# An opening of its own for image 0, and image 3's output stage interleaved with attention's start

## The chip, the cores and the metric

One NeuronCore of a Trainium2 chip runs the whole kernel. Its engines are TensorE (PE in the profile; PEld is its weight load), VectorE (DVE), ScalarE (ACT), GpSimd (POOL) and SyncE (SP), which here only issues DMAs. Each has a queue of its own and executes it in order; semaphores order the engines among each other. The metric is the device time of one execution in microseconds, lower is better.

## The reference

The input is 4 images of 32 x 32 tokens with 384 channels. For each image:

```python
x = x + L0(_gn(x))      # group norm, selective scan layer
x = x + L1(_gn(x))      # group norm, attention

# L0, with DI = 192, N = 16, K = 4 directions, L = 1024 tokens
xh, z = split(x @ in_proj_w.T)
xc    = silu(depthwise_conv3x3(xh) + conv_b)
xs    = [rows, columns, rows reversed, columns reversed] of xc
dts, Bs, Cs = split(einsum(xs, x_proj_w));  dts = softplus(dts @ dt_w + dt_b)
h = h * exp(dt * A) + (dt * u) * B;  y = sum_n(h * C) + D * u      # over 1024 tokens
y = layernorm(sum of the 4 directions) * g + b
return (y * silu(z)) @ out_proj_w.T

# L1: 12 heads of 32, rotary q and k, relative position bias by row and column, softmax, projection
```

All of it is fp32, apart from B/C rows that are split into three bf16 parts.

## The kernel before, in words

Activations lie with channels on partitions and 1024 tokens along the free dimension. PSUM has 8 banks of 512 fp32; `banks(k, n)` names n of them from k. In the scan stage they are `JOB` (0, 1: every matrix product of the input and output stages and of dt), `C_PSUM` (2, 3), `DA` (4, 5) and `Y_PSUM` (6, 7). SBUF is an arena of slots of 1024 columns which are reused.

**Scan stage.** The 4 x 192 rows of (direction, channel) of an image are 6 tiles of 128 (`SEQ`), with 16 states each (`NST`): 96 items per image (`ITEMS`). An item is a pass over the engines: SyncE broadcasts a row of B (`load_b`, L473), GpSimd multiplies by it (`times_b`, L1599, a ring of `R3` = 3), ScalarE computes the decay into `DA` (`decay`, L1442), VectorE scans (`scan`, L1081), TensorE spreads the row of C (`c_product`, L568), VectorE multiplies by it (`times_c`, L1089), and TensorE adds it to `Y_PSUM` (`accumulate`, L577). Softplus for the next tile takes seven ScalarE steps (`soft`, L1410 to L1433) and GpSimd's `delta` (L1576 to L1583) and `times_u` (L1589).

**Front.** The input stage of an image (`front`) is cut into jobs: group norm statistics (`stats`, `moments`, `var`, `rstd`, `norm`), the product `xh` (channels 0 to 127 of xh), `pad` (the remaining 64, as two image halves with padding rows), nine taps of `conv` for either part, the copies `acc` that add conv_b, SiLU in steps `sig` (Exp, Ln, Exp on ScalarE), `cap` and `u` or `gate` on GpSimd, turned copies `ucopy`, the product `z`, and the products `dts` and `bc` of x_dbl, of which B and C are stored and split (`brows`, `bchi`, `split`, `bcmid`, `rest`, `bclo`). **Mid** is the output stage of an image: `y` (three orders added and centred), `yf`, `sq`, `var`, `rstd`, `scale`, `affine`, `gate`, `out` (six half products), `add`, group norm 2, and stores of `x1` and `xn2` to DRAM.

Tables such as `PE_FRONT`, `ACT_MID` give each job of an engine an item at which it is issued into the queue of that engine. For image f the jobs fall into the scan of image f - 1; `*_FIRST` are the tables for image 1, whose jobs fall into image 0's scan, and negative times lie in the scan before that. For image 0 there is no scan to run beside, so each engine runs `in_order(*_FRONT)` for image 0 ahead of its loop, with the same jobs, the same engines and all PSUM uses in `JOB`. SyncE loads x, then eight small columns and `group_mean` on one semaphore (`columns`), `w_in` and the other matrices; TensorE, VectorE and ScalarE wait for all columns at first. `front(0, "next_x")` loads image 1's x after z, `z_store`, `b_store` and `bcs` follow, and only then the first `load_b`.

**The seam.** For image 3 there is no next scan: after the last item each engine runs `in_order(*_MID)` for image 3. Only then attention begins, image by image. Its start follows `START` and `JOBS[0]`: four projections of q and k (`proj`, L561), eight value blocks (`v`, L814, banks 0 to 3), two relative products by column (`rel`, L854) and two by row (`relh`, L843); rotary steps are on VectorE (L1125, L1126) and GpSimd (L1629, L1636). SyncE loads the operands of each head (`operands`, L534) as they get ready. Then come the scores (L880), the biased minimum (L1201), the exponential (L1526), the turning (L891) and the weighing (L905). In the kernel before, SyncE stores x1 and xn2 of image 3 and waits for both before it loads x1 of image 0 and issues head operands.

## Time and profile before

| | us |
|---|---|
| median of 3 runs | 3094.7 (3093.93 to 3096.32) |
| profiled execution | 3094.16 |
| its span | 3092.4 |
| first scan begins | 131.16 |
| last accumulation ends | 1634.97 |
| attention's first scores begin | 1737.13 |
| PE, DVE busy share of the span | 87%, 73% |
| ACT, POOL busy share of the span | 52%, 44% |

The profiled execution took 0.5 us less than the median, and its span is 1.8 us shorter than its time; times below are counted from the start of the span. A timeline row gives the start, the duration, the engine, the line, the operation, what it writes and reads, and in brackets how long the engine had been idle before it and who ended that. In a row that merges several instructions (x12) the duration runs from the first one's start to the last one's end. A fp32 product of 512 columns appears as two matmuls.

### The profile page before, as it was taken

How to read it: one execution, taken by the hardware profiler on the slowest of the kernel's cores; microseconds unless marked ns; L12 is line 12 of the kernel's file. 1: busy time of each engine (PE TensorE's matmuls, PEld its weight loads, DVE VectorE, ACT ScalarE, POOL GpSimd, SP SyncE). 2: the span in 40 equal slices, each digit the busy share in tenths (PEclk: the TensorE clock that was granted, in tenths of full speed). 3: DMA queues.
4: the chain of work that ended last, by engine and by line, in shares of the span. 5: the costliest groups of instructions: out<-in, count | busy, mean ns of one | idle time of the engine just before them, and what ended most of it. 6: DMA issues, size and time to landing. Idle time of an engine off the chain costs nothing. (4 is left out here: it accounts for less than half of the span.)

```text
span 3092.4 us, 40835 instructions
## 1 busy us (share of the span) xinstructions
PE 2684.6 (87%) x16088; PEld 1346.6 (44%) x16088; DVE 2242.5 (73%) x2157; ACT 1614.7 (52%) x1972; POOL 1351.2 (44%) x624
## 2 busy tenths in 40 slices
PE   5579788988889878687767999999999999999999
PEld 2134233333333333232322565555555565556555
DVE  0398988899888998899992566646665566646665
ACT  2464655555555556555541456625564356525564
POOL 1577887887778877788670200011000300011000
PEclk9799999999999999999996999999999999999999
DMA  2344544455444555445551210120120210120110
GB/s 78 108 142 129 163 150 144 150 140 168 165 145 148 142 170 167 154 160 140 197 172 36 76 36 18 39 75 1 36 56 14 63 36 22 35 76 1 35 36 22
DMA packets 93526, 297.03 MB, mean 96 GB/s; under 512 B 16172, under 2 KB 18872, under 8 KB 93208
## 3 DMA queue, kind: packets, MB, share of 16 engines
q1 hardware_dynamic: 93336, 294.43, 30.8%
q8 instruction: 128, 2.10, 0.3%
q14 instruction: 62, 0.51, 0.1%
HBM read 238.27 MB, written 23.07 MB: 85 GB/s over the span
## 5 line engine op out<-in xcount | busy, mean ns | idle before, releaser
L1599 POOL TENSOR_TENSOR arena<-arena 128x1024 f32<-128x1024 f32 x384 | 903.2, 2357 | 307.4 <-DVE arena L1081 297.7
L1081 DVE TENSOR_TENSOR_SCAN arena<-PS,arena 128x1024 f32<-128x1024 f32 x384 | 879.0, 2289 | 102.2 <-ACT PS L1442 70.9
L577 PE MATMUL PS<-arena,ident 128*128 128x512 f32 x1536 | 762.0, 620 | 15.0 <-ACT arena L1453 12.8
L1442 ACT ACTIVATE PS<-arena,a_inf,a_neg 128x1024 f32<-128x1024 f32 x384 | 463.8, 1208 | 586.3 <-DVE arena L1081 580.3
L1201 DVE CUSTOM_DVE_ANT_1 arena<-PS,arena 128x1024 f32<-128x1024 f32 x384 | 467.7, 1219 | 323.4 <-PE PS L880 321.8
L1526 ACT ACTIVATE arena<-arena,neg_max 128x1024 f32<-128x1024 f32 x384 | 441.0, 1148 | 494.8 <-DVE neg_max L1201 494.8
L1089 DVE TENSOR_TENSOR arena<-arena,PS 128x1024 f32<-128x1024 f32 x384 | 460.8, 1200 | 57.7 <-PE PS L568 56.4
L568 PE MATMUL PS<-arena,sel 96*128 96x512 bf16 x768 | 239.4, 394 | 295.5 <-DVE arena L1089 291.7
L1629 POOL TENSOR_TENSOR arena<-arena 128x512 f32<-128x512 f32 x48 | 68.4, 1425 | 955.2 <-ACT arena L1495 955.2
L880 PE MATMUL PS<-arena 64*128 64x512 f32 x1536 | 431.6, 640 | 19.3 <-DMA arena<-arena 12.8
L577 PEld LDWEIGHTS PS<-arena,ident 128*128 128x128 f32 x1536 | 302.5, 198 | 275.0 <-issue 221.4
L891 PE MATMUL PS<-ident,arena 128*128 128x128 f32 x3072 | 414.7, 278 | 3.8 <-ACT arena L1526 3.6
L891 PEld LDWEIGHTS PS<-ident,arena 128*128 128x128 f32 x3072 | 334.9, 142 | 154.9 <-issue 92.5
L568 PEld LDWEIGHTS PS<-arena,sel 96*128 96x128 bf16 x768 | 55.9, 100 | 577.5 <-DVE arena L1089 503.3
L1155 DVE COPY arena<-PS 128x1024 f32<-128x1024 f32 x192 | 233.9, 1218 | 60.6 <-PE PS L891 57.2
L905 PEld LDWEIGHTS PS<-arena 128*32 128x32 f32 x6144 | 157.0, 110 | 134.0 <-issue 131.7
L905 PE MATMUL PS<-arena 128*32 128x128 f32 x6144 | 206.5, 276 | 0.0
L1503 ACT ACTIVATE arena<-PS 128x1024 f32<-128x1024 f32 x192 | 192.7, 1004 | 19.4 <-PE PS L891 19.4
L880 PEld LDWEIGHTS PS<-arena 64*128 64x128 f32 x1536 | 116.5, 185 | 88.5 <-issue 59.0
L1636 POOL TENSOR_TENSOR arena<-arena 128x512 f32<-128x512 f32 x48 | 64.0, 1333 | 176.3 <-DVE arena L1126 175.7
L561 PE MATMUL PS<-normed,arena 128*128 128x512 f32 x288 | 135.7, 615 | 0.6 <-DVE g_tmp L1025 0.6
L577 PE MATMUL PS<-arena 128*128 128x512 f32 (+1 forms) x224 | 108.3, 622 | 12.0 <-ACT arena L1305 5.5
(125 smaller groups left out, 2205.3 us busy)
## 6 DMA issues: line engine op xcount, KB each, us to landing
arena<-b_rows SPq DMA_DIRECT2D x256, 512.0 KB, 3.7
arena<-b_rows SPq DMA_DIRECT2D x256, 256.0 KB, 3.9
arena<-arena SPq DMA_DIRECT2D x192, 128.0 KB, 3.3
arena<-arena SPq DMA_DIRECT2D x120, 64.0 KB, 2.6
normed<-x_in SPq DMA_DIRECT2D x12, 512.0 KB, 5.4
residual<-x_in SPq DMA_DIRECT2D x12, 512.0 KB, 5.6
x<-residual SPq DMA_DIRECT2D x12, 512.0 KB, 5.3
xn<-residual SPq DMA_DIRECT2D x12, 512.0 KB, 4.7
```

The source lines that it names most:

```text
L568: last = pe.matmul(dst[:, half(h)], lhs, rhs(h), start=(k == 0), stop=(k == len(pairs) - 1))
L577: last = pe.matmul(dst[:, half(h)], lhs, rhs[:, half(h)], start=start, stop=stop, skip_group_check=True)
L880: last = pe.matmul(scores_place(s)[:, h * HALF:(h + 1) * HALF], QX[rows, j, qb * P:(qb + 1) * P], KX[rows, j, :], start=True, stop=True)
L891: last = pe.transpose(turned_place(s)[:, t * P:(t + 1) * P], PR[s % 3][:, t * P:(t + 1) * P], idn)
L905: last = pe.matmul(banks(6, 1)[HD * j:HD * j + HD, (n % 2) * P:(n % 2 + 1) * P], V[:, t, head * HD:(head + 1) * HD], PT[:, n % 2, j, t, :] ...
L1081: dve.tensor_tensor_scan(HS[:, at % 2, ::step], DA[:, ::step], DBU[:, at % R3, ::step], 0.0, ALU.mult, ALU.add).then_inc(scan_done.sem, 1)
L1089: dve.tensor_tensor(HC[:, at % R_HC, :], HS[:, at % 2, :], C_PSUM, ALU.mult).then_inc(hc_ready.sem, 1)
L1155: dve.tensor_copy(PT[:, n % 2, s % HG, :, :], turned_place(s).rearrange("p (t q) -> p t q", t=QB)).then_inc(pt_saved[0].sem, 1)
L1201: dve.tensor_tensor_reduce(out=PR[s % 3].rearrange("p (h w) -> p h w", w=IMG), in0=scores_place(s).rearrange("p (h w) -> p h w", w=IMG), i ...
L1442: act.activation(DA, DELTA[:, tile % 2, :], ACT.Exp, bias=a_inf[:, col:col + 1], scale=a_neg[:, col:col + 1]).then_inc(da_ready.sem, 1)
L1526: act.activation(PR[s % 3], PR[s % 3], ACT.Exp, bias=neg_max[:, s % 4:s % 4 + 1], scale=-1.0, accum_out=row_sum[:, qb, at:at + 1]).then_in ...
L1599: pool.tensor_tensor(DBU[:, at % R3, :], DU[:, tile % 2, :], BSB[:, at % R3, :], ALU.mult).then_inc(dbu_ready.sem, 1)
```

## The change

**Image 0's front.** The functions `front` stay, but each engine gets an ordered list instead of the table for image 0 (`PE_BEGIN`, `DVE_BEGIN`, `ACT_BEGIN`). `job_place` puts pad and bc of image 0 in banks 2 and 3, conv and z in banks 4, 5 and 6, 7; xh and dts stay in `JOB`. The waits are made finer: `mean_loaded`, `w_in_loaded`, one increment for each normalised tile, conv 0 waits for XH and conv 1 for XP, the first product of `dts` needs only `U01`. In SyncE's queue group_mean and w_in are ahead of the columns. `prepare_columns` and `negate_a` follow the group norm. The caps, the products `u`, the turned copies, `brows`, `bchi`, `bcmid`, the three `delta` steps and the first `times_u` of image 0 go to VectorE (`begin`). The gate of z (`sig` 2 and 3, `cap` 2 and 3, `gate`) moves into items 1 to 17 of image 0's scan, `bcs`, `next_x` and `z_store` to items 3 and 24 of SyncE's loop. The table for image 1 has its group norm and `xh` two items later, and XH of image 1 also waits for `z_gated`.

**The seam.** For image 0 of attention, TensorE, VectorE and ScalarE run a list each (`PE_BOTH`, `DVE_BOTH`, `ACT_BOTH`) in which numbers are the jobs of attention's start and names with `v` value blocks, and the others are mid jobs of image 3. Value blocks of image 0 use banks 2 and 3 alternately. `zs` of image 3 is in slots 14 and 15 instead of 19 and 20. GpSimd does the gates after its first four rotary halves; SyncE stores x1 ahead of the `rel` operands and xn2 after them, and loads x1 of image 0 last.

The diff, cut to its core:

```diff
-PE_FIRST = {**PE_FRONT, ("stats",): 4, ("xh", 0): 12, ("xh", 1): 12.5, ("xh", 2): 13, ("pad", 0): 21, ("pad", 1): 21.5,
+PE_FIRST = {**PE_FRONT, ("stats",): 6, ("xh", 0): 14, ("xh", 1): 14.5, ("xh", 2): 15, ("pad", 0): 21, ("pad", 1): 21.5,
             ("pad", 2): 22}
...
+ACT_FIRST = {**ACT_FRONT, ("rstd",): 10.2, ("norm", 0): 11, ("norm", 1): 12, ("norm", 2): 13, ("xh",): 17.5, ("pad",): 25,
...
+PE_BEGIN = ([("stats",)] + [("xh", k) for k in range(CT)] + [("pad", k) for k in range(CT)]
+            + [("conv", m, j) for m in range(2) for j in range(9)]
+            + [("dts", 0), ("z", 0, 0), ("z", 0, 1), ("z", 0, 2), ("dts", 1), ("dts", 2), ("dt",),
+               ("bc", 0), ("bc", 1), ("bc", 2), ("z", 1, 0), ("z", 1, 1), ("z", 1, 2)])
+DVE_BEGIN = [("stats", 0), ("stats", 1), ("stats", 2), ("moments",), ("var",), ("columns",), ("cap", 0), ("u", 0),
+             ("ucopy", 0), ("ucopy", 1), ("cap", 1), ("u", 1), ("ucopy", 2), ("ucopy", 3), ("brows",), ("bchi",),
+             ("delta", 0), ("split",), ("bcmid",), ("delta", 1), ("delta", 2), ("times_u",)]
+ACT_BEGIN = ([("rstd",), ("norm", 0), ("norm", 1), ("norm", 2), ("xh",), ("pad",), ("a_neg",), ("acc", 0),
+              ("sig", 0, 0), ("sig", 0, 1), ("sig", 0, 2), ("acc", 1), ("sig", 1, 0), ("sig", 1, 1), ("sig", 1, 2),
+              ("z", 0), ("dts",)] + [("soft", step) for step in range(SOFT_STEPS)] + [("z", 1), ("bclo",)])
+ACT_ZERO = {("sig", 3, 0): 1.5, ("sig", 2, 0): 2, ("sig", 3, 1): 11, ("sig", 3, 2): 11.5, ("sig", 2, 1): 12,
+            ("sig", 2, 2): 12.5}
+POOL_ZERO = {("cap", 3): 5, ("cap", 2): 6, ("gate", 1): 16, ("gate", 0): 17}
+SP_ZERO = {("bcs",): 3, ("next_x", 0): 3.1, ("next_x", 1): 3.2, ("next_x", 2): 3.3, ("z_store",): 24}
...
+        def job_place(f, what, part=0):
+            if f:
+                return JOB
+            return {"pad": banks(2), "conv": (banks(4), banks(6))[part], "z": (banks(4), banks(6))[part],
+                    "bc": banks(2)}[what]
...
+            return slot(14 + j) if m == B - 1 else ZS[:, j, :]
...
+        PE_BOTH = ([0, 1, ("y", 0, 0), ("y", 0, 1), ("y", 0, 2), 2, ("y", 1, 0), ("y", 1, 1), ("y", 1, 2), 3, ("v", 0),
+                    ("var", 0), ("var", 1), ("v", 1), ("v", 2), 4, ("v", 3), ("v", 4), ("out", 0), ("out", 1), 5, ("v", 5),
+                    ("out", 2), ("out", 3), 6, ("out", 4), ("out", 5), 7, ("v", 6), ("stats",), ("v", 7)])
+        DVE_BOTH = ([0, 1, 2, 3, ("scale", 0), ("scale", 1), 4, ("add", 0), ("add", 1), 5, ("add", 2), ("add", 3), 6,
+                     ("add", 4), ("add", 5), ("add", 6), ("moments",), 7, ("var",)])
+        ACT_BOTH = ([0, 1, ("yf", 0), ("sq", 0), 2, ("yf", 1), ("sq", 1), 3, ("v", 0), ("rstd",), ("v", 1), ("v", 2),
+                     ("affine", 0), ("affine", 1), ("v", 3), ("v", 4), ("v", 5), ("v", 6), ("rstd2",), ("v", 7),
+                     ("norm", 0), ("norm", 1), ("norm", 2)])
+        def v_bank(b, t):
+            return banks(t % 4 if b else 2 + t % 2, 1)
...
+            load_mats({"group_mean": KEPT["group_mean"]}, mean_loaded)
+            load_mats({"w_in": SCAN_MATS["w_in"]}, w_in_loaded)
             for name in COLS:
                 sp.dma_start(COL[name][:, :], cols[name]).then_inc(columns.sem, 16)
-            load_mats({"group_mean": KEPT["group_mean"]}, columns)
-            load_mats({"w_in": SCAN_MATS["w_in"]}, first_mats)
...
+                    for job in due(SP_ZERO, i) if b == 0 else ():
+                        front(0, *job)
...
+                    if b == 0 and k == 2:
+                        for part in range(CT):
+                            mid(B - 1, "x1_store", part)
...
+                if b == 0:
+                    for part in range(CT):
+                        mid(B - 1, "xn2_store", part)
+                    sp.wait_ge(x1_stored.sem, x1_stored.at(CT * B))
+                    sp.wait_ge(xn2_stored.sem, xn2_stored.at(CT * B))
+                    load_image(X[:, :, :], x1, b, x_loaded.sem)
...
+                    pe.wait_ge(xn_normed.sem, xn_normed.at(CT * f + k + 1))
...
+                    if j == 0 and f == 0:
+                        ready = (xh_saved, xp_saved)[m]
+                        pe.wait_ge(ready.sem, ready.at(1))
...
+                    if f == 0 and which == 0:
+                        ready = u_ready if k else u_gated
+                        pe.wait_ge(first_mats.sem, first_mats.at(len(SCAN_MATS) - 1))
+                        pe.wait_ge(ready.sem, ready.at(1))
+                    elif f == 0 and k == 0:
...
+                for entry in PE_BOTH if b == 0 else ():
+                    if isinstance(entry, int):
+                        if entry == 2:
+                            pe.wait_ge(y_saved.sem, y_saved.at(3 * B))
+                        job(0, entry)
+                    elif entry[0] == "v":
+                        for k in range(CT):
+                            value_product(entry[1], k)
+                    else:
+                        mid(B - 1, *entry)
+                if b == 0:
+                    pe.wait_ge(gn2_var.sem, gn2_var.at(B))
+                    pe.wait_ge(onehot_loaded.sem, onehot_loaded.at(2 * HG))
...
+                elif what == "cap":
+                    which, = args
+                    dve.wait_ge(sig_exp.sem, sig_exp.at(SIGMOIDS.index(which) + 1))
+                    dve.tensor_scalar(sig_home(which), sig_home(which), EXP_CAP, None, ALU.min
+                                      ).then_inc(sig_capped.sem, 1)
+                elif what == "u":
+                    m, = args
+                    dve.wait_ge(sig_ready.sem, sig_ready.at(m + 1))
+                    dst, src = ((U01[:, 0, :], ACC[:, 0, :]), (ACC[:, 1, 0:HALF], ACC[:, 1, 0:HALF]))[m]
+                    dve.tensor_tensor(dst, src, sig_home(m), ALU.mult).then_inc(u_gated.sem, 1)
...
+                    if k < 2:
+                        dst, src = ((u1[XT:P, :], U01[0:XT, 0, :]), (u2[0:XT, :], U01[XT:P, 0, :]))[k]
+                        dve.tensor_copy(grid(dst), by_column(src))
+                        return
...
+                    if f == 0 and which >= 2:
+                        if which == 3:
+                            act.wait_ge(b_stored.sem, b_stored.at(2))
+                        else:
+                            act.wait_ge(bc_lo.sem, bc_lo.at(1))
...
+                        act.wait_ge(z_gated.sem, z_gated.at(2 * f))
...
-                front(0, *job)
-            for step in range(3):
-                delta(0, step)
-            times_u(0)
+            front(0, "rest")
...
+                    if b == 0 and n == 4:
+                        for job in in_order(POOL_MID):
+                            mid(B - 1, *job)
```

## Rows read from the trace of the kernel before

**Rows 1.** Timeline, end of the opening: start us, us, engine line op, idle before.

```profile
105.76 1.23 DVE L1044 TENSOR_TENSOR arena<-PS,arena 128x1024 f32<-128x1024 f32 x1 [83.90 <-ACT arena L1358]
...
111.27 1.10 ACT L1410 ACTIVATE arena<-PS,dt_b 128x1024 f32<-128x1024 f32 x1
...
121.34 2.34 POOL L1579 TENSOR_TENSOR arena<-arena 128x1024 f32<-128x1024 f32 x1
...
131.16 2.29 DVE L1081 TENSOR_TENSOR_SCAN arena<-PS,arena 128x1024 f32<-128x1024 f32 x1 [23.79 <-POOL arena L1599]
```

**Rows 2.** Timeline, VectorE, two neighbouring scans late in image 3.

```profile
1606.07 2.29 DVE L1081 TENSOR_TENSOR_SCAN arena<-PS,arena 128x1024 f32<-128x1024 f32 x1 [0.16 <-ACT PS L1442]
...
1609.63 2.29 DVE L1081 TENSOR_TENSOR_SCAN arena<-PS,arena 128x1024 f32<-128x1024 f32 x1 [0.16 <-ACT PS L1442]
```

**Rows 3.** Timeline between the last item and attention's first exponential.

```profile
1631.37 3.60 PE L577 MATMUL PS<-arena,ident 128*128 128x512 f32 x8
...
1667.57 24.11 PE L561 MATMUL PS<-arena,w_out 128*128 128x512 f32 x24 [9.52 <-POOL arena L1569]
...
1699.80 3.50 ACT L1260 ACTIVATE residual<-residual,g_bias,g_rstd 128x1024 f32<-128x1024 f32 x3
...
1737.13 2.85 PE L880 MATMUL PS<-arena 64*128 64x512 f32 x12 [0.58 <-ACT arena L1483]
...
1739.58 1.15 ACT L1526 ACTIVATE arena<-arena,neg_max 128x1024 f32<-128x1024 f32 x1 [2.50 <-DVE neg_max L1201]
```

**Rows 4.** Timeline, attention's start in image 1: first projections, first scores.

```profile
2047.98 10.46 PE L561 MATMUL PS<-normed,arena 128*128 128x512 f32 x24
...
2083.66 2.85 PE L880 MATMUL PS<-arena 64*128 64x512 f32 x12 [0.58 <-ACT arena L1483]
```

**Rows 5.** Busy us of each engine in two windows, then PEclk, DMA share, GB/s.

```profile
1652.00:1658.00 6.00, 6.00 (x8) 1.60 (x7) 0.00 (x0) 0.00 (x0) 0.00 (x0) 0.58 0.00 0
...
1740.00:2032.00 292.00, 286.85 (x2845) 170.94 (x2846) 193.94 (x283) 168.40 (x267) 20.14 (x16) 1.00 0.10 27
```

**Rows 6.** Timeline, the opening from the loads to z.

```profile
0.72 1.35 SPq L413 DMA_DIRECT2D normed<-x_in  x3
...
13.30 3.66 DVE L1010 BATCH_NORM_STATS2 bn<-normed 128x6 f32<-128x512 f32 x6 [1.86 <-ACT a_neg L1239]
...
18.16 3.11 PE L586 MATMUL PS<-mv,group_mean 128*128 128x2 f32 x14 [18.16 <-DMA arena<-centre_in]
...
26.71 7.87 PE L577 MATMUL PS<-normed,arena 128*128 128x512 f32 x12 [5.44 <-ACT normed L1260]
...
35.70 3.12 PE L633 MATMUL PS<-normed,arena 128*64 128x480 f32 x24 [1.11 <-ACT arena L1325]
...
40.15 15.09 PE L609 MATMUL PS<-arena 128*128 128x512 f32 x36 [1.34 <-ACT arena L1331]
...
56.44 6.14 PE L609 MATMUL PS<-arena 128*128 128x512 f32 x14 [1.20 <-ACT arena L1268]
...
62.42 1.85 PE L609 MATMUL PS<-arena,last_taps 128*128 128x512 f32 x4
...
65.05 5.42 PE L577 MATMUL PS<-normed,arena 128*128 128x512 f32 x12 [0.78 <-ACT arena L1268]
```

**Rows 7.** Transfers into the tile normed until 25 us, issue to landing.

```profile
DMA to landing us min/median/max: 3.2/4.1/5.8
```

**Rows 8.** Groups by form, VectorE, attention of image 0: busy, mean ns.

```profile
L1172 DVE TENSOR_SCALAR arena<-arena,b_qkv 128x512 f32<-128x512 f32 x5 | 2.4, 487 | 0.2
```

**Rows 9.** Timeline, the gate of image 0's z: Exp on ScalarE, cap on GpSimd.

```profile
83.25 1.06 ACT L1283 ACTIVATE arena<-arena 64x1024 f32<-64x1024 f32 x1
...
84.40 2.76 POOL L1543 TENSOR_SCALAR arena<-arena 64x1024 f32<-64x1024 f32 x1 [9.80 <-ACT arena L1283]
```

**Rows 10.** Page, DMA issues: count, KB each, median us to landing.

```profile
arena<-arena SPq DMA_DIRECT2D x120, 64.0 KB, 2.6
...
x<-residual SPq DMA_DIRECT2D x12, 512.0 KB, 5.3
```

More of the change, by code:

```diff
@@ L661, in front @@
                     c0, rows = ((DI, P), (DI + P, XT))[part]
[L662 removed]
+                    last = add_halves(job_place(f, "z", part)[0:rows, :], W["w_in"][:, k, c0:c0 + rows], XN[:, k, :],
+                                      k == 0, k == CT - 1)
                     if k == CT - 1:
@@ L1090, in times_c @@
                                   ).then_inc(hc_ready.sem, 1)
-            for job in in_order(DVE_FRONT):
-                front(0, *job)
+            for job in DVE_BEGIN:
+                begin(*job)
+            dve.wait_ge(prep.sem, PREPARED_BY - 1)
             dve.wait_ge(consts.sem, consts.at(N_CONST))
@@ L1340, in front @@
                     rows = (P, XT)[part]
-                    act.activation(ZS[0:rows, part, :], JOB[0:rows, :], ACT.Copy).then_inc(z_saved.sem, 1)
+                    act.activation(ZS[0:rows, part, :], job_place(f, "z", part)[0:rows, :], ACT.Copy).then_inc(z_saved.sem, 1)
                 elif what == "acc":
```

222 lines of the change are left out of this document (139 added, 83 removed).

## The prediction

> **What bounds the kernel now.** I read the profile in this order: first the timeline until the first scan, since nothing can overlap a scan stage that has not begun; then two neighbouring items of the scan loop; then the stretch between the last scan and the first attention scores; last the busy time and the granted clock of a few windows.
>
> The loop of 4 x 96 items starts with the scan of item 0 at 131.16 us, after VectorE was idle for 23.79 us; everything before it is the serial opening of image 0 [rows 1]. In the loop an item takes 3.56 us (two scan starts): decay on ScalarE, scan 2.29 and the product with C on VectorE, 0.16 us of waiting [rows 2]. It is a cycle of its own: a later first scan shifts everything behind it by as much, so the opening counts one for one. TensorE's last accumulation ends at 1631.37 + 3.60 = 1634.97, and attention's first scores begin at 1737.13, its first exponential at 1739.58 [rows 3]: 102.2 us in which the output stage of image 3 runs first and attention's start second. There the 24 output matmuls take 24.11 us [rows 3], against 10.46 us for 24 projections of image 1 [rows 4]: in the window 1652 to 1658 the granted clock averages 0.58, TensorE drops from 2.4 to 1.2 GHz [rows 5]. Attention itself keeps TensorE busy 286.85 of 292 us at clock 1.00 [rows 5]; the edit leaves it alone.
>
> **Part A, the opening.** The chain before ran through all of the front: each PSUM use waited for ScalarE to empty JOB, and SiLU steps went ScalarE, GpSimd, ScalarE, GpSimd. I rebuild it step by step with the new order, in us from the start of the span:
> - Loads. The third x tile is issued near 1.6 and lands at most 5.8 later, at 7.4 [rows 6, 7]. Before, VectorE waited until the small columns and group_mean had landed too and began its statistics at 13.30 [rows 6]. They now follow each tile: the last third of 3.66 us ends at 8.7. Moments take the 1.2 us that lie between the statistics' end and the first matmul: 9.9. I keep the 3.11 us of the statistics matmuls: 13.0. The matrices are issued right behind x, some 4 us earlier than now, so I let nothing wait for them; a miss costs about 1 us.
> - The gap 18.16 + 3.11 to 26.71 is 5.4 us of variance, root and three normalisations; TensorE now waits for one of three (3.50 / 3 = 1.2 each, [rows 3] has the same line in the later norm), so 5.4 - 2.3 = 3.1: 16.1. Product xh 7.87 (its first matmuls slow, kept): 24.0. Pad 3.12: 27.1; it needs no wait, as it has banks of its own, and saving XH lies beside it. Convolution 0, 15.09: 42.2; saving XP falls beside it. Convolution 1, 6.14 + 1.85 = 8.0, again in banks of its own: 50.2 [rows 6].
> - SiLU of half 0 runs beside convolution 1: bias copy 1.1, Exp 1.1, cap, Ln 1.1, Exp 1.1, product 1.2 from 42.2, ready at 48.7 with a cap of 0.9. The first x_dbl product (a third of 5.42) then runs at once: 52.0. z part 0 (12 matmuls, 5.42): 57.4. Beside it SiLU of half 1 and the four turned copies, now on VectorE. VectorE's full-width TENSOR_TENSOR takes 1.23 us [rows 1]; no row shows its copy from SBUF with turned strides. The nearest is TENSOR_SCALAR on half the length, 0.49 us [rows 8]. Lower bound 0.5 us for each half length, upper bound 1.23 for each full one. From convolution 1's end at 50.2: copy, Exp, cap, Ln, Exp, product, halves of 0.5 to 0.7, give 54.0; the copies of half 1 add 1.4 to 2.8: 55.4 to 56.8. Both lie under 57.4, so z hides them and the term is 0; I take the upper bound, as strides can only slow a copy. Without this cover they would cost up to 3 us.
> - The other two thirds of x_dbl 3.6: 61.0. Copy 1.1: 62.1. dt product 1.8: 63.9. Softplus 121.34 - 111.27 = 10.1 [rows 1]: 74.0. The B/C product (5.4) runs beside it until 69.3, then VectorE has brows, bchi, delta 0 and split at 1.23 each: 74.2; bcmid 1.2: 75.4; delta 1, delta 2, times_u, 3 x 1.2: 79.0. On GpSimd three such products cost 2.34 each [rows 1]. The first product with B stays on GpSimd, 2.34: 81.4. The B rows are stored from 70.5 on, and land before 79. z part 1, bclo and the bcs loads end near 83, when the product with C of item 0 asks for them behind scan 1: no wait of size.
>
> First scan at 81.4 instead of 131.16: **49.8 us**. The Trainium skill ("VectorE: DVE Perf Modes", the perf-mode tier table) says that a copy or tensor_scalar of fp32 from SBUF runs at two elements a cycle and any PSUM source at one. The 0.49 us for 512 agrees; by it the turned copies take their lower bound and, being hidden, change nothing, while bcmid ends 0.6 us sooner, which would give 50.4.
>
> **What the opening gives back.** Gate z of image 0 is not removed but moved into items 1 to 17: on ScalarE six passes of 1.06, on GpSimd two caps of 2.76 [rows 9] and two products of 2.34. ScalarE's decay (1.2) must follow each scan at once, so an item holds 3.56 us of its work. Items 11 and 12 get decay 1.2, Ln and Exp 2.2, and a normalisation of 1.2 for image 1: 4.6, so 1.0 over, twice. Elsewhere it fits. GpSimd runs up to two items ahead: 6 us of slack; the caps fall in items slowed by statistics, the products right behind the four delta products, where I count a lag of 5.4 to 5.8, just covered. XH of image 1 now also waits for these gates, ScalarE's decay being next in its queue; by my count 0.4 us to spare. bcs and next_x stand before the fourth B load on SyncE's queue, which may cost 0 to 3. I take 3 in all, bounds 2 and 12. Part A: 49.8 - 3 = **47**.
>
> **Part B, the seam.** TensorE gets one list with both works, and banks 2, 3 for values, so I sum its work. Attention's start alone takes 2083.66 - 2047.98 = 35.7 us in image 1, at full clock [rows 4]. To it come two y products as z's, 2 x 5.42; variance, 8 matmuls of 0.45, 3.6; 24 output matmuls 10.5; statistics 1.6 (half of the 3.11 at 1.2 GHz). Sum 62.2, so it ends at 1697.2, and the last value copy gives scores at 1697.7.
>
> Is the dependent chain shorter? y 0 ends at 1645.9, its square 2.0 later; projection 2 covers that. y 1 ends at 1654.2, variance at 1662.5. Ln and Exp on PSUM 2.1, scale 1.2, affine 1.25 twice with a value copy ahead, gates 2 x 2.32 on GpSimd: yg_ready at 1672.9. TensorE has v 1, v 2, rel 0, v 3, v 4 meanwhile and arrives at 1673.3. So it holds with 0.4 us in hand, and a microsecond more in that chain is a microsecond lost. Behind the output products the statistics end at 1695, and ScalarE must do three normalisations (3.50, [rows 3]) before its first exponential: 1697.7 + 3.5 = 1701.2 instead of 1739.58. That, not the scores, sets the gain: 38.4, **38**. In the queue of SyncE the three x1 stores stand before the eight rel loads of heads 0 to 3; the last store is released at the sixth addition, about 1690.8, and a load of 64 KB lands in 2.6 us, a store in 5.3 [rows 10]. So head 0 is there near 1694 to 1697, under TensorE's arrival, and the norms wait for the store until 1696.2, also under it. zs moves to other slots and costs nothing.
>
> Sum: 47 + 38 = 85. The profiled execution took 3094.16 us, 0.5 below the median of 3094.7, so 3094.7 - 85 = 3009.7, say **3010**.
>
> **Rivals.**
> (1) The deferred gates and the SyncE order cost more than 3 us in the item loop. If none of it is covered: ScalarE 6.5, GpSimd 10.2 minus what the slack takes, up to 15: **3022**. For it: GpSimd's lag is within 1 us of its slack. Against: at most two items overflow on ScalarE by my count.
> (2) The seam's side work ends last: rel loads behind x1 stores, or the gate chain. Each has under 1 us in hand, and loads share the queues with 1.5 MB of stores: 3 to 8 us, **3015**.
> (3) TensorE's clock drops in the seam as before. From 1653 on some 43 us of work at 2.4 GHz remain; at 1.2 GHz part B brings nothing: **3048**. For it: the row at 0.58 [rows 5]. Against: before it came two pauses of 2 us per 5.4 of work; the new list has none.
> (4) Slower than before: attention of image 0 starts at the lower level and stays there. Its 286.85 busy us [rows 5] would double; it decides once more than 85 us of it run at 1.2 GHz, and in full gives **3297**. Against: the clock was back at 1.00 in that window after a far longer drop.
> (5) Opening shorter than summed, as statistics matmuls and xh run warm and x lands at 4 us: **3001**.
>
> **How the numbers follow.** Chances: forecast 0.60, (1) 0.13, (2) 0.12, (3) 0.05, (4) 0.02, (5) 0.08. Range 2998 to 3028: it takes in the upper bound of the give-back, (1), (2) and (5), and leaves out (3) and (4) and tails. A measurement tells 0.2%, 6 us; all but (4) lie far below, faster 0.97, same 0.01, slower 0.02.
>
> **What would show it.** First scan at 80 to 83; TensorE nearly without gaps from 16 to 61 at clock 1.00; VectorE idle on ScalarE around items 11 and 12, 1 us each. Scans of image 1 begin 45 to 49 us sooner. From the last accumulation to the first exponential 66 us instead of 104.6, granted clock 1.00 throughout, the first output product 38 us behind it. It would be wrong if a window there shows 0.5, if the first scores wait for a DMA, or if item times above 3.6 add up to more than 12 us in image 0.

## The result, and where the time went

The changed kernel took 3015.28 us (median of 4 runs, 3011.24 to 3019.43) against 3095.51 us of the kernel before on the same chip (3093.93 to 3096.33): ratio 0.9741, 95% interval 0.9725 to 0.9758, 80 us faster. The forecast was 3010 us, range 2998 to 3028. Its profiled execution took 3011.24 us with a span of 3009.5. Two later sets of runs of the same kernel gave 3018.14 (0.9753, interval 0.9739 to 0.9768) and 3016.24 (0.9763, interval 0.975 to 0.9777).

The profiled executions differ by 82.9 us. The scans mark off the stretches; the times are differences of starts in the timelines:

| stretch | before | after | saved |
|---|---|---|---|
| start of the span to the first scan | 131.16 | 82.40 | 48.8 |
| image 0's scan stage | 370.82 | 374.75 | -3.9 |
| images 1 and 2 | 763.92 | 759.11 | 4.8 |
| image 3, to its last scan | 361.56 | 361.52 | 0.0 |
| last scan to attention's first exponential | 112.12 | 78.54 | 33.6 |
| first exponential to the end | 1352.82 | 1353.18 | -0.4 |

The 4.8 us of images 1 and 2 are not the edit's, as shown below. Without them the change is worth 78 us: 45 of 47 forecast in the opening, 33.6 of 38 in the seam.

The opening after, timeline, all engines; columns as in [rows 1]:

```profile
10.48 3.12 PE L636 MATMUL PS<-mv,group_mean 128*128 128x2 f32 x14 [10.48 <-DVE mv L1160]
...
16.86 7.68 PE L627 MATMUL PS<-normed,arena 128*128 128x512 f32 x12 [3.26 <-ACT normed L1401]
...
24.47 3.12 PE L686 MATMUL PS<-normed,arena 128*64 128x480 f32 x24
...
27.51 20.96 PE L659 MATMUL PS<-arena 128*128 128x512 f32 x50
...
51.72 5.31 PE L627 MATMUL PS<-normed,arena 128*128 128x512 f32 x12
...
54.18 0.86 DVE L1117 COPY arena<-arena 64x512 f32<-64x512 f32 x2
...
55.05 1.23 DVE L1119 COPY arena<-arena 64x512 f32<-64x512 f32 x2
...
73.67 0.69 DVE L1130 CAST arena<-arena 128x1024 bf16<-128x1024 f32 x1
...
74.44 3.03 POOL L1711 TENSOR_TENSOR arena<-arena 128x1024 f32<-128x1024 f32 x1 [74.02 <-DVE arena L1130]
75.61 2.95 DVE L1143 TENSOR_TENSOR arena<-arena 128x1024 f32<-128x1024 f32 x1
...
82.40 2.29 DVE L1225 TENSOR_TENSOR_SCAN arena<-PS,arena 128x1024 f32<-128x1024 f32 x1
```

TensorE goes from product xh to pad and to all 54 tap matmuls (50 in the row shown, 4 behind it) with no idle bracket; in [rows 6] pad and both convolutions had a bracket of 1.1 to 1.3 us that named ScalarE. The turned copies end at 56.28, before z does at 57.03. The oddity is the pair at 74.44 and 75.61: VectorE's `delta` 2 took 2.95 us where its other full-width products took 1.23 [rows 1], and GpSimd's subtraction 3.03 where it took 2.34.

The seam, by windows of the same work: the end of the last accumulation to the first exponential, kernel before, then after. Columns: length, busy us of PE, PEld, DVE, ACT, POOL with counts, PEclk (1.00 is 2.4 GHz, 0.50 is 1.2 GHz), DMA share, GB/s.

```profile
1635.00:1739.60 104.60, 84.75 (x282) 39.35 (x282) 26.94 (x38) 21.57 (x30) 17.26 (x10) 0.76 0.24 76
```

```profile
1585.30:1656.30 71.00, 69.83 (x282) 34.98 (x281) 25.35 (x38) 21.28 (x29) 17.24 (x10) 0.95 0.28 75
```

This pair is the seam in one look. TensorE has 282 matmuls in both. Its idle time fell from 104.60 - 84.75 = 19.9 us to 1.2, which is 18.7 of the 33.6 gained. The other 14.9 are busy time of the same matmuls, which a clock of 0.95 instead of 0.76 shortened: the pauses had cost their own length and, as I read it, the clock behind them. The clock is still not at 1.00, and this is most of what made 33.6 of the forecast's 38. PE rows of the seam after, and ScalarE's at its end:

```profile
1611.71 4.14 PE L883 MATMUL PS<-arena,normed 128*128 128x384 f32 x12
1615.68 3.92 PE L923 MATMUL PS<-arena 128*128 128x32 f32 x32
1619.42 5.55 PE L883 MATMUL PS<-arena,normed 128*128 128x384 f32 x12
1624.81 4.18 PE L611 MATMUL PS<-arena,w_out 128*128 128x512 f32 x8
1628.92 3.77 PE L923 MATMUL PS<-arena 128*128 128x32 f32 x32
1632.51 3.87 PE L883 MATMUL PS<-arena,normed 128*128 128x384 f32 x6
...
1653.28 2.03 PE L949 MATMUL PS<-arena 64*128 64x512 f32 x8 [0.78 <-ACT arena L1632]
...
1652.92 3.49 ACT L1401 ACTIVATE residual<-residual,g_bias,g_rstd 128x1024 f32<-128x1024 f32 x3
...
1656.32 1.13 ACT L1682 ACTIVATE arena<-arena,neg_max 128x1024 f32<-128x1024 f32 x1
```

```profile
1615.70:1618.90 3.20, 3.20 (x31) 3.20 (x29) 0.62 (x1) 2.75 (x3) 1.26 (x1) 1.00 0.11 41
1618.90:1622.30 3.40, 3.40 (x9) 2.19 (x9) 0.69 (x1) 0.00 (x0) 3.40 (x2) 0.50 0.00 0
...
1633.00:1636.20 3.20, 3.20 (x6) 1.62 (x5) 0.41 (x1) 0.00 (x0) 0.00 (x0) 0.53 0.00 0
1636.20:1653.00 16.80, 16.30 (x107) 7.56 (x105) 8.41 (x20) 2.61 (x9) 0.00 (x0) 1.00 0.50 141
```

Two value blocks (L883) are too long: 5.55 instead of 4.14 us for 12, 3.87 instead of 2.2 for 6. Each stands right behind a column-wise relative block (L923, 32 matmuls of 32 columns), and in each the granted clock is 0.50, with TensorE busy in every part of the window. The first fall came at 1618.90, with the last narrow matmuls of the block. "Busy" is a weak word here: idle time under 0.15 us gets no bracket, and the narrow matmuls follow each other every 0.11 us where 384 columns take 0.33. In the kernel before these 32-column matmuls were woven, four at a time, between value matmuls; in the list of the seam each block runs in one piece.

### The profile page after: what moved, and what is told of

Read it like the earlier page. It is cut to its first block and busy times, and to the rows that moved or that the text cites. A ratio compares the mean times of both kernels' runs of the same rounds, so it can differ in the third digit from the quotient of the medians.

```text
span 3009.5 us, 40839 instructions
## 1 busy us (share of the span) xinstructions
PE 2660.0 (88%) x16088; PEld 1337.4 (44%) x16088; DVE 2259.1 (75%) x2174; ACT 1603.2 (53%) x1962; POOL 1334.7 (44%) x616
## 5 line engine op out<-in xcount | busy, mean ns | idle before, releaser
L1298 DVE COPY arena<-PS 128x1024 f32<-128x1024 f32 x192 | 233.8, 1218 | 60.9 <-PE PS L960 57.4
```

## Experiments

Times in this section, unless said otherwise, come from the profiled execution, cut at the scans as above.

**Do the two parts stand alone?** Each part was taken alone. `opening_only` is the changed kernel with the old seam (a), `seam_only` the old kernel with the new seam (b):

```diff
 (a)
+            for job in in_order(PE_MID):
+                mid(B - 1, *job)
...
-                for m, blocks in START if b else ():
+                for m, blocks in START:
 (b)
-            for job in in_order(PE_MID):
-                mid(B - 1, *job)
...
+                for entry in PE_BOTH if b == 0 else ():
...
-                for m, blocks in START:
+                for m, blocks in START if b else ():
```

> The opening, the table for image 1 and the moved gates as in the changed kernel, the seam as before. If the two parts add up: 48.8 us at the first scan, minus 3.9 in image 0's scan, so about 3050 us (ratio 0.9855), with the seam at 104.6 us from the last accumulation to the first exponential and its granted clock falling to 0.50 again. Rival: the 4.8 us that images 1 and 2 were shorter in the changed kernel belong to the opening's shift; then the same items 63 to 67 of image 1 and 71, 84 of image 2 are shorter here and the time is near 3045. If they are a matter of when TensorE's clock happens to drop, these items differ from run to run.

Measured: 3050.24 us (ratio 0.9857, interval 0.9842 to 0.9872), 44 us below before; first scan at 82.38, image 0's stage 375.33, last scan to first exponential 109.38.

> The opening as before, the seam as in the changed kernel. If the parts add up: 33.6 us from the last scan to the first exponential, so about 3062 us (ratio 0.989), first scan at 131.2. In the seam the granted clock should drop to 0.50 twice for 2 to 3 us, each time behind a block of 32 narrow matmuls of a rel job, if those blocks are the cause; if the drops come from a moment in time they fall elsewhere or not at all. If image 1 and 2 stay at 385 and 379 us, the 4.8 us go with the opening; if they are shorter here too, they are spread between runs.

Measured: 3056.31 us (0.9878, interval 0.9862 to 0.9895), 38 us below before; first scan 129.82, image 0's stage 370.55, last scan to first exponential 75.18. 44 + 38 = 82 against 76 to 80 for both: they add, with a remainder of 2 to 6 us. The profiles show two parts of it. In `opening_only` the old seam took 109.38 instead of 112.12 us, 2.7 less, since its long stretch at half clock (0.50 from 1615.7 to 1660.1, in the kernel before from 1653.0 to 1704.2) was 7 us shorter; and `seam_only` had a seam without a fall of the clock. The longer stage of image 0 belongs to the opening alone. The seam by itself was 3.4 us shorter than within the change: here the same unbroken blocks ran with the clock at 1.00.

`after_again` is the changed kernel once more, in the same set:

> The changed kernel once more. Its four runs lay between 3011.2 and 3019.4 us, the one with a profile being the fastest. Theory: the opening (first scan 82.4) and the seam (71.0 us) repeat within 0.5 us, and the spread lies in the scan stage of images 1 and 2, in which TensorE's clock drops at varying items: a slower run shows it there, with a lower mean clock. Rival: the spread lies in the seam, whose two clock drops are long in some runs and short in others; then the seam of this profile differs from 71.0.

Measured: 3018.14 us. First scan 83.03, image 0's stage 375.35, seam 76.86, images 1 and 2 385.26 and 381.13 us instead of 382.42 and 376.69. The same kernel thus differs by 7.3 us in images 1 and 2, which is the 4.8 us above. One item of image 1, the changed kernel's first profile, then `after_again`:

```profile
709.94 1.88 PE L627 MATMUL PS<-arena,ident 128*128 128x512 f32 x4
...
709.90:711.90 2.00, 1.92 (x5) 0.58 (x4) 2.00 (x2) 0.00 (x0) 2.00 (x2) 1.00 0.61 229
```

```profile
713.76 3.62 PE L627 MATMUL PS<-arena,ident 128*128 128x512 f32 x4
...
713.70:717.40 3.70, 3.70 (x6) 1.31 (x5) 3.27 (x5) 1.86 (x6) 3.70 (x2) 0.50 0.87 225
```

The four accumulating matmuls took 3.62 us at 1.2 GHz instead of 1.88 at 2.4 GHz, and the item 4.89 instead of 3.80. The clock falls at such items of an image in some executions and not in others; it did in the kernel before as well (image 1 385.17, image 2 378.75). So nothing in images 1 and 2 is counted for or against the edit.

**Why is the seam 5 us longer than summed?** My theory: the clock falls behind 32 narrow matmuls in a row. The rival: the side chain or the loads of head 0 end last (the prediction's rival 2), and the clock only fills time that would be waited anyway. `seam_mix` weaves the relative blocks into value blocks again and shifts value blocks toward them:

```diff
-                    ("var", 0), ("var", 1), ("v", 1), ("v", 2), 4, ("v", 3), ("v", 4), ("out", 0), ("out", 1), 5, ("v", 5),
-                    ("out", 2), ("out", 3), 6, ("out", 4), ("out", 5), 7, ("v", 6), ("stats",), ("v", 7)])
+                    ("var", 0), ("var", 1), ("v", 1), ("v", 2), ("job", 4, (3, 4)), ("out", 0), ("out", 1),
+                    ("job", 5, (5, 6)), ("out", 2), ("out", 3), 6, ("out", 4), ("out", 5), 7, ("v", 7), ("stats",)])
```

> In the seam the value blocks 3 and 4 are woven between the lines of rel 0, and 5 and 6 between those of rel 1, as in the later images, and v 7 comes ahead of the statistics with its copy ahead of the normalisation. Theory: unbroken runs of matmuls with 32 moving columns let the clock fall, though TensorE is busy throughout; woven it stays at 1.00, v 3 and v 4 take 3.9 instead of 5.4 us and v 5 1.9 instead of 3.7: 3.3 us less, and 0.6 from the copy that no longer stands ahead of the norms, the seam at about 67.1 us, the time some 3.9 us below the changed kernel. Rival: the drops come from the moment or from what stands ahead of the rel blocks; then they stay, and only the 0.6 us is gained.

Measured: 3019.77 us (0.9756, interval 0.9741 to 0.977), seam 76.53. The clock was 1.00 through both blocks, as the theory has it, but the gain did not arrive. The chain of waits of `seam_mix` (start, us, what) and its PE rows there:

```profile
1651.78 0.70 DVE residual L1207
...
1652.50 0.32 SPq L462
...
1654.80 5.44 DMA arena<-arena
...
1660.28 3.70 PE PS L949 x8
```

```profile
1654.87 1.69 PE L636 MATMUL PS<-mv,group_mean 128*128 128x2 f32 x14
1657.24 2.08 PE L949 MATMUL PS<-arena 64*128 64x512 f32 x4 [0.67 <-DVE g_tmp L1170]
1660.28 3.70 PE L949 MATMUL PS<-arena 64*128 64x512 f32 x8 [0.96 <-DMA arena<-arena]
```

The last addition (L1207) releases the last x1 store on SyncE's queue (L462), behind which the `rel` loads of the heads stand; one issued at 1654.80 landed 5.44 us later, scores waited 0.96 us for it, and ran at half clock (3.70 us for 8, 2.03 in the seam above). That is a part of rival 2 at work, once the time in front of it shrinks. It costs behind the first exponential, a stretch that took 1355.59 us here and 1353.18 in the change. It does not set the seam's length of 76.53: the first exponential began at 1661.86, as the three norms ended (1658.45 + 3.51), and these follow the statistics. This edit had also put value block 7 ahead of the statistics, which made them 1.9 us later (62.05 us behind the last accumulation, 60.12 in `seam_mix2`). `seam_mix2` keeps the weaving, leaves blocks 6 and 7 where they were and puts the loads ahead of the stores:

```diff
-                    ("var", 0), ("var", 1), ("v", 1), ("v", 2), 4, ("v", 3), ("v", 4), ("out", 0), ("out", 1), 5, ("v", 5),
+                    ("var", 0), ("var", 1), ("v", 1), ("v", 2), ("job", 4, (3, 4)), ("out", 0), ("out", 1), ("job", 5, (5,)),
...
-                    if b == 0 and k == 2:
-                        for part in range(CT):
-                            mid(B - 1, "x1_store", part)
...
                 if b == 0:
+                    for part in range(CT):
+                        mid(B - 1, "x1_store", part)
```

> Seam alone changed against the changed kernel: v 3 and v 4 woven into rel 0, v 5 into rel 1, the rest of TensorE's order as it was, and SyncE issues the rel operands ahead of the three x1 stores. Theory: both losses of seam_mix go. No clock drop: last scan to first exponential 75.2 us, as in the run of the seam alone that had no drop, against 76.9 and 78.5 in the two of the changed kernel. No wait of the first scores for a DMA, so the stretch behind the first exponential returns from 1355.6 to about 1353. Rival: the rel operands land late for another reason (their own issue, 0.8 us each for 8), then the wait stays; or the norms wait for the later stores and the first exponential moves by 1 to 3 us.

Measured: 3017.57 us (0.976, interval 0.9745 to 0.9775), seam 75.17. Windows over its two woven blocks, and its first scores:

```profile
1622.00:1632.00 10.00, 10.00 (x52) 6.91 (x50) 2.40 (x3) 3.73 (x5) 4.66 (x2) 1.00 0.06 22
1634.00:1642.00 8.00, 8.00 (x44) 5.31 (x42) 1.98 (x3) 0.49 (x1) 0.00 (x0) 1.00 0.00 0
...
1657.30 2.85 PE L948 MATMUL PS<-arena 64*128 64x512 f32 x12 [0.78 <-ACT arena L1633]
```

No window below 1.00, no DMA in a bracket. The seam is 3.4 us shorter than in the change, the theory's amount, and as long as in `seam_only`, which has the stores ahead of the loads: the order of the stores did nothing for it. The stretch behind the first exponential took 1354.28 instead of the 1353 that I expected. The median shows no gain; images 1 and 2 happened to be the long kind again (385.16, 381.13).

The rival form of the theory is that the seam, not the block, is special. `plain_rel` therefore unweaves the blocks at the start of attention's images 1 to 3, and leaves the seam alone:

```diff
-        START = [(m, ()) for m in range(4)] + [(None, (0, 1)), (4, (2, 3)), (5, (4, 5)), (6, ()), (7, ()),
+        START = [(m, ()) for m in range(4)] + [(None, (0, 1)), (4, ()), (None, (2, 3)), (5, ()), (None, (4, 5)), (6, ()), (7, ()),
```

> The changed kernel, but in images 1 to 3 the value blocks stand behind the two rel jobs instead of between their lines: the same matmuls in another order, six more unbroken blocks of 32 narrow matmuls. If unbroken narrow blocks let the clock fall, some of the six are followed by a stretch at 0.50 (in the seam it was two of two, one of two and none of two), and each such drop costs 1.5 to 2 us; attention's start in these images had none in any profile. If the seam's drops came from something else in the seam, all six stay at 1.00.

Measured: 3013.73 us in one run, which says nothing at this size. Of the six unbroken blocks in images 1 to 3 one was followed by the drop (0.50 from 2328.3 to 2331.7):

```profile
2324.89 3.75 PE L923 MATMUL PS<-arena 128*128 128x32 f32 x32
2328.46 5.73 PE L883 MATMUL PS<-arena,normed 128*128 128x384 f32 x12
```

In the new seam, by kernel, one profiled execution each:

| seam | kernels | blocks followed by a drop |
|---|---|---|
| 78.54 | the change, plain_rel, rest_on_dve | 2 of 2 each |
| 78.54 | after_third | 1 of 2, 6.8 us long (value block 7.03 us) |
| 76.86 | after_again, warm, gates_early | 1 of 2 each |
| 75.18 | seam_only | 0 of 2 |
| 75.17 | woven: seam_mix2, all_four | 0 of 2 each |
| 76.53 | woven: seam_mix, with the late statistics | 0 of 2 |

The length of the seam follows the drops: one stretch of 3.4 us at half clock adds 1.7 us, two such stretches or the long one of `after_third` add 3.4. An unbroken block makes a drop possible, not certain (10 of 16 in the seam, 1 of 6 elsewhere); none came at a woven one. What it is in the block that lets the clock fall was not tested: the narrowness, or gaps too short for a bracket.

**What did the last microsecond of the opening cost?** The stretched pair at 74.44 and 75.61 suggests that GpSimd and VectorE keep each other from SBUF. `rest_on_dve` gives the subtraction to VectorE, in front of the products:

```diff
-             ("delta", 0), ("split",), ("bcmid",), ("delta", 1), ("delta", 2), ("times_u",)]
+             ("delta", 0), ("split",), ("bcmid",), ("rest",), ("delta", 1), ("delta", 2), ("times_u",)]
...
+                elif what == "rest":
+                    dve.wait_ge(bc_mid.sem, bc_mid.at(1))
+                    dve.tensor_tensor(REST, REST, BCP[:, 1, :], ALU.subtract).then_inc(bc_last.sem, 1)
...
-            front(0, "rest")
```

> Image 0's second subtraction for the bf16 parts (rest) goes from GpSimd to VectorE, ahead of delta 1. In the changed kernel GpSimd ran it from 74.44 to 77.47 while VectorE's delta 2 took 2.95 us instead of 1.22. Theory: the two slow each other when both read and write SBUF; alone on VectorE, rest and delta 2 take 1.2 each, and the first scan comes 0.5 to 0.8 us earlier, at 81.7. Rival: delta 2 is slow for another reason; it stays near 2.95 and the first scan comes 1.2 us later, at 83.6.

Measured: 3013.9 us in one run; first scan at 81.11, 1.3 us sooner than in the change. Most of that is the front's: its pad matmuls began at 23.63 instead of 24.47, and that start varies from 23.61 to 25.09 among the kernels whose front is unchanged. From the pad matmuls to the first scan these take 57.9 us (82.40 - 24.47 = 57.93; the change run again 57.94 twice), and `rest_on_dve` 81.11 - 23.63 = 57.48: 0.45 us sooner, with one instruction more on VectorE.

```profile
73.56 1.23 DVE L1133 TENSOR_TENSOR arena<-arena 128x1024 f32<-128x1024 f32 x1
74.70 1.22 DVE L1142 TENSOR_TENSOR arena<-arena 128x1024 f32<-128x1024 f32 x1
...
76.03 1.23 DVE L1146 TENSOR_TENSOR arena<-arena 128x1024 f32<-128x1024 f32 x1
...
81.11 2.29 DVE L1228 TENSOR_TENSOR_SCAN arena<-PS,arena 128x1024 f32<-128x1024 f32 x1
```

With the other engine still, `delta` 2 (L1146) took 1.23 again, 1.7 less, of which the added instruction takes back 1.2. The Trainium skill ("SBUF — State Buffer", section "SBUF: two separate sides") says that a VectorE operation with two SBUF inputs and a GpSimd one that reads SBUF take turns over a shared pair of ports, each for the whole instruction. The rows of the change agree for VectorE: 75.61 + 2.95 - 1.22 = 77.34, within 0.2 us of the end of GpSimd's instruction at 77.47. GpSimd's loss, 0.7 us, is smaller than the 1.06 us for which the product before it (74.28, 1.22 us) still ran; no run here shows why.

**Can the slow first matmuls be warmed?** `warm` adds matmuls on zeros whose results nothing reads, six products while x is loading and three behind the statistics:

```diff
+            def keep_warm(n):
+                for _ in range(n):
+                    pe.matmul(banks(2, 1), XP[:, 0:P], XP[:, 0:HALF], start=True, stop=True, skip_group_check=True)
...
+            keep_warm(6)
...
+                if job == ("stats",):
+                    keep_warm(3)
```

> Six matmuls of zeros into banks 2 before TensorE's first wait and three between the statistics and xh; results unused. Theory: the statistics' 3.12 us and the slow start of xh (7.68 instead of 5.3) are TensorE at 1.2 GHz after idling, and can be bought back with work in the idle time: statistics near 1.7, xh near 5.3, first scan 3.8 us earlier, 78.6. Rival: matmuls on zeros, or so early, do not raise the clock, or three of them outlast the gap: no gain, or up to 1.5 us lost.

```profile
1.68 6.93 PE L846 MATMUL PS<-arena 128*128 128x512 f32 x12 [1.68 <-DVE arena L1088]
10.43 2.07 PE L636 MATMUL PS<-mv,group_mean 128*128 128x2 f32 x14 [1.82 <-DVE mv L1168]
12.37 5.47 PE L846 MATMUL PS<-arena 128*128 128x512 f32 x6
17.62 5.71 PE L627 MATMUL PS<-normed,arena 128*128 128x512 f32 x12
```

For comparison, windows of the change over its statistics matmuls and the slow start of xh:

```profile
10.48:13.60 3.12, 3.11 (x14) 3.03 (x14) 0.00 (x0) 0.00 (x0) 0.00 (x0) 1.00 0.98 333
16.86:20.00 3.14, 3.14 (x4) 1.48 (x5) 0.00 (x0) 2.11 (x2) 0.00 (x0) 1.00 0.89 252
```

Measured: 3013.8 us (0.9743, interval 0.9726 to 0.9759), first scan at 81.2, 1.2 us sooner than in the change where I had expected 3.8; the pad matmuls began at 23.27, barely ahead of the 23.61 to 25.09 of unchanged fronts. The first group did its work: statistics matmuls 2.07 instead of 3.12. Then the clock fell all the same, to 0.50 from 11.6 to 18.4: behind 1.82 us without matmuls, during the two-column ones, and before the three fillers began at 12.37. So these ran at 1.2 GHz themselves, took 5.47 us and outlasted the gap that they were to fill, and xh began at 17.62 instead of 16.86. It made up for that with 5.71 instead of 7.68. The theory's "at 1.2 GHz" is not what the record of the clock says of the change, as the two windows above read 1.00; only the spacing of the matmuls speaks for it (xh 0.85 us apart at first, 0.43 at its end, the latter as in other stretches at 1.00).

**Is the give-back in items 11 and 12?** Two scans of the change with more than 0.9 us of idle time before them, and what ScalarE did:

```profile
126.86 1.06 ACT L1435 ACTIVATE arena<-arena 64x1024 f32<-64x1024 f32 x1
127.82 1.23 ACT L1401 ACTIVATE normed<-normed,g_bias,g_rstd 128x1024 f32<-128x1024 f32 x1
128.95 1.19 ACT L1589 ACTIVATE PS<-arena,a_inf,a_neg 128x1024 f32<-128x1024 f32 x1
...
130.18 2.29 DVE L1225 TENSOR_TENSOR_SCAN arena<-PS,arena 128x1024 f32<-128x1024 f32 x1 [0.99 <-ACT PS L1589]
...
134.57 2.29 DVE L1225 TENSOR_TENSOR_SCAN arena<-PS,arena 128x1024 f32<-128x1024 f32 x1 [0.99 <-ACT PS L1589]
```

Ln, Exp and the norm end at 128.95, so the decay is 0.82 us late, twice. `gates_early` moves the four steps to items with room:

```diff
-ACT_ZERO = {("sig", 3, 0): 1.5, ("sig", 2, 0): 2, ("sig", 3, 1): 11, ("sig", 3, 2): 11.5, ("sig", 2, 1): 12,
-            ("sig", 2, 2): 12.5}
+ACT_ZERO = {("sig", 3, 0): 1.5, ("sig", 2, 0): 2, ("sig", 3, 1): 5, ("sig", 3, 2): 7, ("sig", 2, 1): 8,
+            ("sig", 2, 2): 9}
```

> ScalarE's Ln and Exp of image 0's z gate go from items 11 and 12, where each met a normalisation of image 1, to items 5, 7, 8 and 9, which hold one softplus step each. Theory: items 11 and 12 return from 4.39 to 3.57 us, 1.65 us in all, and no other item grows, since decay 1.2 + softplus step 1.1 + gate step 1.1 = 3.5 stays under 3.57; image 0's scan goes from 374.7 to 375.6 (seven runs) to near 373.1. Rival: 3.5 of 3.57 does not fit once the waits between the steps are counted, and items 5, 7, 8, 9 take what 11 and 12 give.

Measured: 3018.98 us in one run, image 0's stage 375.57: no shorter, against the 373.1 that I expected. By pieces, as us above 3.565 for each item:

| items | before | after | after_third | gates_early | warm |
|---|---|---|---|---|---|
| 0 to 23 | 4.8 | 6.95 | 6.89 | 5.31 | 7.56 |
| 35 to 41 | 2.89 | 4.60 | 4.58 | 6.28 | 2.89 |

Items 0 to 23 came down by 1.6, as the two overflows say. Items 35 to 41, in which this edit moves nothing, rose by 1.7: in this execution the clock fell twice there, to 0.50 from 217 and again from 234 us, in `after` once. The rise of 1.7 against before goes with such a fall too: `warm`, with the same jobs, had none there and has 2.89. But it is the usual case: ten of the eleven profiles with the new opening have at least 4.58 in these items, the two with the old opening 2.89, so it counts as a price of the change, though nothing shows why the clock falls there. In items 0 to 23 the falls from 106 to 137 us play no part: `after_third` had none of them, and the same 6.9. (Why `warm` has 7.56 there, with item 3 at 4.89 instead of 4.50, was not followed up.) The 2.15 us there are not all gates. The two overflows are 1.65. Another 0.93 comes from the table of image 1: its three pairs of statistics moved from items 0, 1, 2 to items 2, 3, 4, and the first had stood in item 0, where the time of the missing product with C was free (kernel before, then the change):

```profile
133.37 1.26 DVE L1010 BATCH_NORM_STATS2 bn<-normed 128x6 f32<-128x512 f32 x2
134.73 2.29 DVE L1081 TENSOR_TENSOR_SCAN arena<-PS,arena 128x1024 f32<-128x1024 f32 x1
```

```profile
92.86 1.28 DVE L1153 BATCH_NORM_STATS2 bn<-normed 128x6 f32<-128x512 f32 x2
```

Items slowed by statistics took 4.51 and 5.56 us before and 4.52, 4.50 and 5.55 after. The rest, -0.48, is item 4 of the kernel before, 4.05 us, which took 3.57 in `seam_only`, the kernel with the same old opening. So the 3.9 us given back are about 1.65 of gates, 0.9 of statistics and 1.7 that go with the clock, less 0.5.

**All four edits.** `all_four` joins `seam_mix2`, `rest_on_dve`, `warm` and `gates_early`; `after_third` is the change beside it on the same chip.

> seam_mix2, gates_early, rest_on_dve and warm together. If they add: 1.2 (rest) + 1.2 (warm) + 1.65 (gates) + 1.7 to 3.4 (seam, against runs with one or two clock drops) = 5.8 to 7.5 us under the changed kernel, near 3009 against the kernel before at 3094. Rival: the drop of TensorE's clock only moves elsewhere, as the stretch behind the first exponential was 1354.3 instead of 1353.2 in seam_mix2, and the sum is 3 to 4 us.

> The changed kernel beside all_four on the same chip. By its eight runs so far 3011 to 3022 us, with the seam at 75.2 (no drop), 76.9 (one) or 78.5 us (two) and images 1 and 2 together 759.1 or 766.4 us by the profile. It is what all_four's gain is taken from.

Measured: 3007.62 us (3006.04 to 3008.49; 0.9727, interval 0.9714 to 0.974) against 3016.24 (3014.67 to 3021.91). The two sets do not overlap: 8.6 us by the medians. Of the spans' difference, 3012.9 - 3005.8 = 7.1, the opening has 2.7 (first scan at 78.82 instead of 81.55; 2.3 of it ahead of the pad matmuls, at 21.34 instead of 23.61, where the three fillers took 4.52 us instead of the 5.47 in `warm` and xh 5.31, and 0.45 the subtraction), image 0 has 1.1 (373.34 instead of 374.45; its items 0 to 23 have 5.53 in place of 6.89), the seam 3.4 (75.17 instead of 78.54): 7.2. Images 1 to 3 (3.8 less) and attention behind (3.9 more) cancel; attention varies so between runs of one kernel (1351.2 to 1355.0 in the three profiles of the change), images 1 and 2 by more. `all_four` beats both kernels.

## Why the prediction was right, and where its terms were off

The forecast case came true: both parts, nearly in full, 3015.28 against 3010.

**The opening, step by step.** Forecast and measured end of each: statistics 8.7 and 9.27; statistics matmuls 13.0 and 13.6; start of xh 16.1 and 16.86; xh 24.0 and 24.5; all of convolution 50.2 and 50.2; turned copies 56.8 and 56.28; z part 0 57.4 and 57.0; softplus 74.0 and 73.6; first scan 81.4 and 82.40. Two errors cancel until softplus: the front started 0.8 late and ran 1.2 faster. The term that failed is "delta 1, delta 2, times_u, 3 x 1.2": `delta` 2 cost 2.95 beside GpSimd. [rows 1] gave a price for a product on each engine, but one taken without looking at what the other engine did. A loss of 1.7 us there was partly made up by an earlier start, 74.3 instead of 75.4. Part A by the first scan is 48.8 instead of 49.8.

The tier rule of the Trainium skill ("VectorE: DVE Perf Modes", the perf-mode tier table): CAST L1130 (`bcmid`) took 0.69 us, about half the 1.23 that I took, and so did the full-width cap, as the rule says; `bcmid` took some 0.5 less. The turned copies did not go by it, and the upper bound was the right half of the choice: two of 64x1024 took 2.10, and of the two short kinds the plain one (L1117) took 0.43 each and the turned one (L1119) 0.62. The four short copies took 2.10 together; the "1.4 to 2.8" of the forecast does not follow from its own bounds, which give 2.0 to 2.5. z hid all of them, so the term was 0 as forecast.

**The give-back.** Forecast 3, measured 3.9, with one mechanism named in advance (items 11 and 12, 0.82 each against 1.0). That the sum came out near is partly luck: 1.7 of it goes with the clock in items 35 to 41 and 0.9 with image 1's statistics two items later, and no step of mine had either, and the 0 to 3 us set aside for the order of SyncE's queue were not seen. GpSimd's lag stayed covered and rival 1 did not occur.

**The seam.** Forecast 66.2 us from the end of the last accumulation to the first exponential, measured 1656.32 - 1585.28 = 71.04. The first output product began 1624.81 - 1585.28 = 39.5 behind, forecast 38, so the gate chain held. The order of the end was right: statistics, then three norms (3.49 us), then the exponential. The step that failed is "Attention's start alone takes 2083.66 - 2047.98 = 35.7 us in image 1, at full clock": the sum priced all of attention's start from [rows 4], where the relative blocks are woven, while the new list runs them in one piece, and rival 3 was dismissed with "the new list has none", meaning pauses. There were none that the rows show, and the clock fell nonetheless: 78.54 - 75.18 = 3.4 us. The remaining 1.5 us are about what the output matmuls add, which take 4.1 us for eight or 0.52 each instead of the 0.44 of [rows 4], also in `seam_mix2` at clock 1.00 (4.26 to 4.29). What slows them was not tested. The statistics took 1.70 where I had halved 3.11 "at 1.2 GHz" to 1.6; the size is right, but no row shows that clock over the 3.11, as said above under `warm`. Two of the forecast's own signs of being wrong came up, windows at 0.50 and a score that waited for a DMA, so its "granted clock 1.00 throughout" failed although the time came out. The third sign, more than 12 us of item time above 3.6 in image 0, could tell nothing: the kernel before has 27 us of it already, the change 31.

The Trainium skill ("TensorE: Matmul & The Clock Gate", section "HAM oscillation — how this bites in real kernels") explains a falling clock by waits between bursts of matmuls. The kernel before agrees: three pauses of 2 us up to 1651.76, and 0.58 after them [rows 5]. The seam of the change differs as far as its rows can tell: TensorE has no idle bracket before 1618.90, where the clock falls, and there the measurement decides.

**Rival 2** was priced at 3 to 8 us and did not decide in the change, where a head's load held TensorE for only 0.39 us at 1655.70. `seam_mix` shows that it stood right behind: with the list shortened, a load held the scores for 0.96 us. **Rival 4** did not occur: attention took 1353.18 against 1352.82. **Rival 5** did not occur: the first x tile was there at 4.14, but the statistics of the last began at 7.98, after a wait for its DMA, where I had 7.4.

What stays open: why an unbroken block is followed by the drop in one execution and not in the next; what in the block does it; why the clock falls at some items of images 0 to 2; and the 0.52 us of the output matmuls.

## What to carry to other kernels

When two serial stages are merged into one TensorE list, price the merged list with rows in which the instructions stand in the same order; a stage's row with narrow matmuls woven in does not price the same matmuls in one piece, and weaving them cost nothing here. When work moves from one of GpSimd and VectorE to the other, write down what both do at each moment, and count two SBUF-to-SBUF products at once as in turn. And when a stretch shrinks, look at the queue behind it (here stores ahead of loads): the next wait came as soon as a few us were gained.

## What the runs showed of the hardware

- TensorE's granted clock fell to 0.50 (1.2 GHz) with no idle bracket before it, at the end of 32 matmuls of 32 columns in a row (3.66 to 4.14 us): 10 of 16 times in the seam, 1 of 6 in other places, 0 of 6 in the seams with the same matmuls woven, 4 to 12 at a time, between value matmuls. A drop cost 1.7 us, the long one of `after_third` 3.4.
- After 6.93 us of matmuls on zeros (`warm`) the 14 two-column matmuls took 2.07 instead of 3.12 us (1.69 in `all_four`). The clock still fell at 11.6, during these, and was 0.50 until 18.4 although three more fillers ran from 12.37 on.
- At the start of the execution the recorded clock reads 1.00 while matmuls of 512 columns follow each other every 0.85 us instead of 0.43 (16.86 to 20.00 in the change).
- VectorE TENSOR_TENSOR 128x1024, fp32, beside a GpSimd one: 2.95 us instead of 1.22, and GpSimd 3.03 instead of 2.34.
- VectorE copies in SBUF, fp32: plain 64x512 0.43 us, with turned strides 0.62, turned 64x1024 1.05 (2.10 for two); a cast of 128x1024 to bf16 0.69.
- One and the same kernel's images 1 and 2 took 759.1 or 766.4 us, by whether the clock fell at single items of the scan loop.
